# Attention in units of up to four batches, with the key mask added to the bias on GpSimd in layers one and three

## The reference, cut to what matters

```python
q = (xn @ Wq).reshape(b, n, HEADS, DIM_HEAD).transpose(0, 2, 1, 3)
k, v = (kv[..., :DIM_HEAD], kv[..., DIM_HEAD:])      # null key and value put in front
sim = jnp.einsum('bhid,bjd->bhij', q, k) * SCALE + attn_bias   # one bias for all batches
sim = jnp.where(causal, neg, sim)
sim = jnp.where(m, sim, neg)                          # m: key mask of the batch
attn = jax.nn.softmax(sim, axis=-1)
out = jnp.einsum('bhij,bjd->bhid', attn, v)
```

## Time and profile before

| | us |
|---|---|
| median of three runs | 2393.82 |
| lowest, highest | 2392.82, 2397.09 |
| the profiled execution | 2392.7 |
| its span | 2390.2 |

### The profile page before, as it was taken

The page is one execution under the profiler, slowest core; times in us unless marked ns, Lnnn a source line. Parts: engine busy times, 40 slices in busy tenths (PEclk is TensorE's granted clock), DMA queues, the critical chain, the costliest instruction groups (busy, mean ns, idle before and its releaser), DMA issues. The chain is left out here.

```text
span 2390.2 us, 47281 instructions
## 1 busy us (share of the span) xinstructions
PE 2071.5 (87%) x16272; PEld 1454.0 (61%) x16273; DVE 1118.4 (47%) x3373; ACT 995.8 (42%) x2622; POOL 589.3 (25%) x970
## 2 busy tenths in 40 slices
PE   6899999787999996899967765996889999959994
PEld 3477777654777775566644544883557776736663
DVE  5388882354888823201043336106568884321122
ACT  2388871155887721111113221213567783112221
POOL 2022120176111115211132332015811111321111
PEclk9999999998999997899968985997989999979997
DMA  2274422002533121422132332641010003131113
GB/s 80 77 217 132 142 66 93 0 1 62 151 93 92 55 72 40 141 99 99 54 105 92 126 104 96 203 139 36 0 48 20 20 11 142 36 123 46 44 44 114
DMA packets 157135, 197.91 MB, mean 83 GB/s; under 512 B 15315, under 2 KB 130223, under 8 KB 156941
## 3 DMA queue, kind: packets, MB, share of 16 engines
q1 hardware_dynamic: 145228, 169.09, 22.7%
q0 software_dynamic: 11712, 26.26, 3.1%
HBM read 120.60 MB, written 88.90 MB: 88 GB/s over the span
## 5 line engine op out<-in xcount | busy, mean ns | idle before, releaser
L938 ACT ACTIVATE att_pr<-all_h,att_nmax 128x128 f32<-128x128 f32 (+3 forms) x768 | 422.1, 552 | 93.2 <-DVE att_nmax L894 92.0
L996 PEld LDWEIGHTS att_t_ps<-all_ident,att_pr 64*128 64x128 f32 x3840 | 184.0, 139 | 108.6 <-issue 43.3
L996 PE MATMUL att_t_ps<-all_ident,att_pr 64*128 64x64 f32 x3840 | 188.5, 224 | 10.9 <-DVE att_pt L902 10.1
L874 POOL COPY att_rexp<-att_rinv 128x512 f32<-128x512 f32 x96 | 58.6, 610 | 515.7 <-DVE att_rinv L906 515.7
L1164 PE MATMUL out_y_ps<-outw_wo,mem_qt 128*128 128x256 f32 x768 | 179.2, 387 | 0.0
L902 DVE COPY att_pt<-att_t_ps 128x256 f32<-128x256 f32 (+3 forms) x240 | 177.3, 739 | 1.0 <-PE att_t_ps L996 1.0
L1786 PE MATMUL exp_f_h_ps<-exp_f_xs_t,cw_f_w 128*128 128x512 f32 (+1 forms) x512 | 172.5, 496 | 1.5 <-DVE exp_f_xs_t L1823 1.5
L1798 PE MATMUL exp_f_y_ps<-cw_f_w,exp_f_hid 128*128 128x256 f32 x768 | 168.4, 379 | 0.0
L1164 PEld LDWEIGHTS out_y_ps<-outw_wo,mem_qt 128*128 128x128 f32 x768 | 144.5, 193 | 25.4 <-issue 6.8
L1798 PEld LDWEIGHTS exp_f_y_ps<-cw_f_w,exp_f_hid 128*128 128x128 f32 x768 | 144.8, 190 | 19.5 <-issue 0.5
L1853 ACT ACTIVATE exp_f_hid<-exp_f_h_ps 128x512 f32<-128x512 f32 (+1 forms) x128 | 62.3, 490 | 222.2 <-PE exp_f_h_ps L1786 222.2
(11 more groups left out here) (395 smaller groups left out, 3886.1 us busy)
## 6 DMA issues: line engine op xcount, KB each, us to landing
sorted_c<-all_zero SPq DMA_DIRECT2D x8, 2056.0 KB, 13.1
sorted_f<-all_zero SPq DMA_DIRECT2D x8, 2056.0 KB, 11.3
cw_f_w<-in_L_ffn_w_dram SPq DMA_DIRECT2D x16, 1024.0 KB, 8.1
cw_f_w<-in_L_ffn_W_dram SPq DMA_DIRECT2D x16, 1024.0 KB, 8.5
com_f_rows<-expert_f SPq DMA_DIRECT2D x20, 512.0 KB, 6.9
band<-rev SPq DMA_DIRECT2D x2, 4096.0 KB, 18.6
att_bias<-band SPq DMA_DIRECT2D x32, 256.0 KB, 3.1
til_c_xs<-sorted_c SPq DMA_DIRECT2D x40, 128.5 KB, 2.1
```

The costliest lines, as they stand in the source:

```text
L874: pool.tensor_copy(rexp[:], group_ap(rinv, G).unsqueeze(3).to_broadcast([P, B, 2, DH])).then_inc(rexp_ready, 1)
L938: nc.scalar.activation(pr[p % 4][:, hh, 0:n], sc[p % 4][:, hh, 0:n], ACT.Exp, scale=-1.0, bias=nmax[:, b, q, h:h + 1], accum_out=rsum[:, b ...
L996: last = nc.tensor.transpose(t_ps[e % 2][:, n, (q + 1) * hh + kb, :], pr[p % 4][d, hh, P * kb:P * (kb + 1)], c.ident[d, d])
```

## The change

Steps become units (first, i, q, b, n) of n batches, with n = 4, 2, 1, 1 for q = 0, 1, 2, 3, so that each holds 512 score columns per head, or 384 for q = 2. A round has 11 units instead of 16 steps; the offsets in the loops stay as they are, counted in units. Reduces, exponentials, transposes and value matmuls keep their number and size; copies of transposed tiles are one per unit. Waits on `s_read` and `p_ready` count single (batch, head) items.

The mask matmul covers a whole unit; its stationary operand `lead` is one in rows 0 and 64 and zero elsewhere, and `kmask` now holds the mask in all 128 rows. In layers 1 and 3 this matmul is left only in units of q = 3. For the others GpSimd writes bias + mask into one of four new buffers `bm`, two instructions per unit, and VectorE reads `bm` in place of the bias, behind a new wait on `masked`. GpSimd's adds stand in its queue as follows: units 5, 6, 7, 8 of the round ahead of L867 of the q = 3 group, units 9 and 10 behind L867 of the q = 1 group, the next round's unit 0 ahead of L867 of the q = 2 group. The buffer `rb_sb` is doubled in layer 0. The loading and clearing of the mask change as the diff shows.

```diff
-        self.all_loaded = 16 * (7 + (2 if self.cosine else 0))
+        self.all_loaded = 16 * (6 + (2 if self.cosine else 0))
-        for n in range(2):
-            sp.dma_start(self.mask_w[DH * n:DH * n + 1, :], self.mask.rearrange("b s -> (b s)").rearrange("(a n) -> a n", a=1)).then_inc(loaded, 16)
+        sp.dma_start(self.mask_w[:], row(self.mask.rearrange("b s -> (b s)"))).then_inc(loaded, 16)
...
-        pool.memset(c.kmask[:], 0.0).then_inc(cleared, 1)
...
-            dve.wait_ge(cleared, 1)
-            for n in range(2):
-                at = slice(DH * n, DH * n + 1)
-                link(nc.vector.tensor_scalar(c.kmask[at, :, :], mask_u[at, :].rearrange("a (b s) -> a b s", b=B), 1.0, -NEG,
-                                             ALU.subtract, ALU.mult))
+            link(nc.vector.tensor_scalar(c.kmask[:], mask_u.rearrange("p (b s) -> p b s", b=B), 1.0, -NEG, ALU.subtract, ALU.mult))
...
+    TOGETHER = (4, 2, 1, 1)
     NG = HP * QT
-    NP = NG * B
+    units = [(B * (QT * i + j) + b, i, q, b, TOGETHER[q]) for i in range(HP) for j, q in enumerate(ORDER) for b in range(0, B, TOGETHER[q])]
+    NU = len(units)
+    last_of = [max(u for u in range(NU) if units[u][0] // B == G) for G in range(NG)]
+    group_after = {u: G for G, u in enumerate(last_of)}
...
+    POOL_MASKED = (0, 1, 2) if cosine else ()
+    BM = 4
+    RB = 1 if cosine else 2
+    PER_ROUND = NU // HP
+    POOL_MASKED_AT = ((), (5, 6, 7, 8), (), (PER_ROUND,))
+    MASKED_WITHIN = ((), (), (9, 10), ())
...
+            def mask_bias(u):
+                first, i, q, b, n = units[u]
+                keys = P * (q + 1)
+                if causal_select:
+                    pool.wait_ge(bias_ready, 2 * (first // B + 1))
+                elif first % ROUND == 0:
+                    pool.wait_ge(bias_loaded[i % 2][0], 32 * (i // 2 + 1))
+                if masked_number[u] >= BM:
+                    pool.wait_ge(s_read, items(masked_units[masked_number[u] - BM], 1))
+                for hh in range(2):
+                    out = bm[masked_number[u] % BM][:, hh, 0:keys * n].rearrange("p (b n) -> p b n", b=n)
+                    pool.tensor_tensor(out, bias_ap(i, q, hh).unsqueeze(1).to_broadcast([P, n, keys]), c.kmask[:, b:b + n, 0:keys],
+                                       ALU.add).then_inc(masked, 1)
...
             for G in range(NG):
                 if G + 2 < NG:
-                    i, q, _ = steps[B * (G + 2)]
-                    select(i, q)
+                    select(*group(G + 2))
+                if POOL_MASKED:
+                    mask_ahead(G, POOL_MASKED_AT)
                 pool.wait_ge(s_read, 2 * B * (G + 1))
                 pool.tensor_tensor(group_ap(c.p_null, G), group_ap(nmax, G), group_ap(c.nsn, G), ALU.subtract).then_inc(null_less, 1)
+                if POOL_MASKED:
+                    mask_ahead(G, MASKED_WITHIN)
                 pool.wait_ge(null_ready, G + 1)
...
+                    if u in masked_number:
+                        dve.wait_ge(masked, 2 * masked_number[u] + hh + 1)
+                    for k in range(n):
+                        at = slice(keys * k, keys * (k + 1))
+                        add = bm[masked_number[u] % BM][:, hh, at] if u in masked_number else bias_ap(i, q, hh)
...
+            _, _, q, b, n = units[u]
+            return q == 0 or b // n % 2 == 1
...
-            for p in range(NP + 4):
-                if p < NP:
-                    exponentials(p)
-                if p < NP and p % B == B - 1:
-                    null_keys(p // B)
-                if 2 <= p < NP + 2 and not taken_by_vector(p - 2):
-                    take_pt(p - 2)
-                if p % B == 3 and p > B:
-                    take_rb(p // B - 1)
+            for u in range(NU + 4):
+                if u < NU:
+                    exponentials(u)
+                if u in group_after:
+                    null_keys(group_after[u])
+                if 2 <= u < NU + 2 and not taken_by_vector(u - 2):
+                    take_pt(u - 2)
+                if u - 4 in group_after:
+                    take_rb(group_after[u - 4])
...
+                    if u not in masked_number:
+                        nc.tensor.matmul(s_ps[bank % 3][:, 0:keys * n].rearrange("p (b n) -> p b n", b=n), c.lead[d, :], c.kmask[d, b:b + n, 0:keys],
+                                         start=True, stop=False)
```

## The result

The changed kernel takes **2500.6 us** (median of four runs, 2495.5 to 2504.9) against 2395.4 for the kernel before beside it. The ratio is 1.0439, with a 95% interval of 1.0413 to 1.0466. It is slower, and by about as much as forecast (2488). The profiled execution took 2504.9 us, its span is 2503.1.

A forecast was written before the change was run, and what follows sets the result against it. TensorE was taken to set the attention stages' pace. Layer 0 +17.5, layers 1 and 3 +39.1 each, and -1 in front gave +94.7 us on 2392.7, thus a 2488 us median; range 2365 to 2540.

The forecast's parts named there:

- the three waits: New attention waits: at the lone q=0 unit, in VectorE's queue at the last q=3 unit, and behind GpSimd's adds.
- Fewer steps and masks: TensorE per round: 11 steps for 16 and fewer waits save 1.35 us; with masks gone in layers 1 and 3, 2.75.
- Wait 1: Lone q=0 unit: TensorE's transposes need ScalarE's copy queued behind L943, which waits for GpSimd; 2.3 us, 2.7 in layer 0.
- Wait 2: Last q=3 unit's step: VectorE's reduces and output product delay the copy TensorE needs; 0.9 us of stall.
- the late add: Layers 1 and 3: unit 5's second add holds VectorE's second reduce 0.8 us, making Wait 2 cost 1.7.
- The 0.4 us behind the q=0 reduces: TensorE stall of 0.4 us where unit 8's copy stands behind VectorE's 2.2 us of q=0 reduces.
- Wait 3: Layers 1 and 3: GpSimd's 8.6 us add burst holds q=3's L943; ScalarE idle 6.3, TensorE waiting 2.1 for row-sum copy.
- late copies: Layers 1 and 3, behind GpSimd's burst: late exponentials and copies cost 0.5 and 1.2 us two and three steps later.
- The rival on the clock: Stalls halve TensorE's clock for some 8 us, losing 4 us in 21 rounds: +84, total 2571; chance 0.08.
- The ends of the stages: Attention starts: -3 us per layer, +1.2 for the first add in layers 1 and 3; -1 in front of attention.
- The waits were not absorbed: Rival for attention: free VectorE and ScalarE time absorbs the waits, -63 us, about 2330; chance 0.21 including half-absorbed forms.
- The adds were not cheap: Rival for GpSimd's adds: 0.61 us for 512 columns, 4.4 us burst, total 2421; decides below some 0.8; chance 0.17.

The follow-up runs named there:

- e8: Changed kernel with single steps (16 per round) instead of larger units, GpSimd's mask adds spread over the groups in layers 1 and 3; ratio 0.9996 to the kernel before.
- e6: Changed kernel with q=0 in two units of two batches instead of one of four, queue order kept; ratio 1.0078 to the kernel before.
- e11: Changed kernel with q=0 in two units, masks by matmul without GpSimd adds, VectorE's tile copy before the output product; 2357.0 us, ratio 0.9848 to the kernel before.
- e3: Changed kernel without GpSimd's adds, all units getting their mask by matmul; ratio 1.0216 to the kernel before.
- e4: Changed kernel without any mask for q=0, 1 and 2 in layers 1 and 3, neither adds nor matmuls; ratio 1.0227 to the kernel before.
- e1: Changed kernel with ScalarE's transposed-tile copy ahead of the null-key exponential; ratio 1.0203 to the kernel before.
- e2: Changed kernel with GpSimd's adds for units 5 to 8 behind its q=3 null-key subtraction instead of ahead; ratio 1.0287 to the kernel before.
- e7: Changed kernel with the edits of e1 and e2, plus VectorE's tile copy ahead of the output product; ratio 0.9979 to the kernel before.

## Why the prediction was right

The mechanism of the three waits was right, shown by the experiments above. That the sum came so near is in part luck, because one term was missing and others were too large. The changed kernel's row of layer 1 shows it:

```profile
640.00:900.00 260.00, 213.74 (x2962) 152.91 (x2958) 175.66 (x546) 169.71 (x538) 127.33 (x209) 0.95 0.29 79
```

In these 7.06 rounds TensorE is idle for 260 - 213.74 = 46.3 us, 6.6 per round, where the forecast's new waits add up to 8.2. The clock costs 1.7 per round, which the forecast left out. The remaining 28.6 stand against 28.2. So the waits, too long by 1.6 us, stood in for the clock. Over the whole kernel the falls of the clock make 31 us; without them the time would be near 2470 us, an estimate, and the forecast 18 us too high instead of 13 too low.

**What bounds the kernel.** The pace was read rightly, and so was the spacing of steps. That TensorE sets the pace of the kernel before was neither shown nor refuted: e8 was meant to test it, but took only some 0.4 us of work per round off TensorE and added as much in waits. In the changed kernel the waits set it, as the forecast said.

**Fewer steps and masks** (-1.35 and -2.75 us per round). The first is borne out by e6 and e11: 12 instead of 16 steps give -0.7 in layer 0 (e6) and -1.2 in layers 1 and 3 (e11), with four steps saved rather than five and some waits left. One reading in it was off: the 0.76 us at 698.96 is the wait of the weight load, while the matmuls waited 0.36 us. The part of 1.4 us for the masks was mis-sized. It took the distance from the mask's start to the scores' start as the price; e3 against e4 gives 0.65 us per round for the large units, e8 some 0.4 for single steps.

**Wait 1** was forecast at 2.3 us per round in layers 1 and 3, and TensorE waited 2.08; in layer 0, forecast 2.7, 18.1 us in seven waits are 2.6. e1 and e6 show the cause: the copy behind the null keys, and the lone unit. What the step missed was the clock behind it.

**Wait 2** was forecast at 0.9, with the late add 1.7; measured 1.56 in layer 1. In e1 it is 0.93 with the burst in the same place, and in e2 1.63 with the burst moved, so the late add is not shown as the cause of the larger value. The same row in layer 0 is 10.4 us in 15 waits of both kinds, 1.3 per round, as the sum of 0.9 and 0.4. e7 removes it. The 0.4 us behind the q=0 reduces stood at 0.49 (the transposes at 692.14).

**Wait 3:** the adds took 1158 and 917 ns, where 1190 and 950 were taken from the broadcast row; their burst 8.0 us, forecast 8.6. ScalarE waited 6.36 us for a forecast 6.3. TensorE's wait for the row-sum copy was 1.21, not 2.1: that term was too large, probably since TensorE itself came later, slowed by what went before. The row of turned sums waited 1.1 us (7.7 us in 7 waits), and the forecast had 1.2 for late copies. But that match is chance: in layer 0, with no burst, the row waits just as long (7.6 us in 7), where 0.3 was charged, and in e2, with the burst moved, still 0.6.

**The rival on the clock** came half true, and this is the term that was missing. I gave a falling clock 0.08 and 4 us per round. It fell behind every q=0 stall of layers 1 and 3 and behind four of seven in layer 0, but each time only for some 4 us, at 1.7 us of full clock. The Trainium skill (TensorE: Matmul & The Clock Gate, Part 1) has the rule that idle time brings the half clock; the windows from 696 agree, with TensorE busy for 1.29 and 0.63 of 2 us and the clock then at 0.50. A stall of this length does not always bring it down: three stalls of 2.6 us in layer 0 left it at 1.00.

**The ends of the stages** come out near their forecast together: layer 0 gained 23.5 us from first to last score matmul where the pace alone makes 7.75 x 3.34 = 25.9, so the start gave back 2.4 of the 3 us; in layer 1 the pace makes 45.0 of the measured 44.2, against a net gain of 1.8 forecast. Outside attention 1.5 us remain.

**The other rivals.** The waits were not absorbed, though three engines had idle time. The adds were not cheap: 1.16 us, well above the 0.8 from which that rival decides.

The signs that the prediction named were 8.5 and 9.1 us per group (8.62 and 9.21), null keys waiting 3 to 4 us at q=0 (5.2, too low a forecast) and 6 at q=3 (6.4), and the two copies.

## What to carry to other kernels

Before steps are merged, write each in-order queue beside the others and look for a short instruction that waits for a result of the group before: if a group shrinks to one step, its distance to that result shrinks with it, and all that stands behind it pays. Work moved to an idle engine costs by what it stands ahead of, not by its length, and where it can stand neither ahead nor behind without somebody waiting it is better left where it was, as the run without adds shows. And the price of an instruction on a pipelined engine is not the distance from its start to the next one's start: compare the whole step with it and without it. Here 0.18 us read off the rows were worth 0.07.

## What the runs showed of the hardware

- A stall of TensorE of 2.1 us, in a stretch where it was busy for 1.92 of 4 us, was followed by about 4 us with a granted clock of 0.50 to 0.87, 1.7 us of full clock lost. Every such fall read in the changed kernel, e2, e3, e4 and e6 cost 1.7 us within 0.1. Not every stall brought one: seven of seven of 2.1 us did in layer 1 of the changed kernel, four of seven of 2.6 us in its layer 0, one of seven in layer 0 of e3. In e1, whose single waits in layer 1 from 620 us on are at most 1.1 us long, except for one of 1.8, the clock stayed at 1.00.
- A matmul of 384 columns (bfloat16) that starts a bank's accumulation in front of float32 scores lengthened the step by 0.07 us, although the scores started 0.17 us behind it; for 512 columns it was 0.12 to 0.13 us.
- GpSimd adds float32 and bfloat16 with a broadcast operand in 430 ns for 128 columns (e8), 917 for 384 and 1158 for 512, about 1.9 ns per column and 0.2 us fixed. Beside the adds VectorE's reduces kept their 0.48 us for 256 columns (480 ns in the mean in the changed kernel and in e3, which has no adds), so no contention shows.
